# Two small attentions with scores two tiles ahead, and an fp4 layer with shared copies and another order

## The chip, the cores and the metric

One Trainium2 chip, of which the kernel uses one core. A core has TensorE (PE in the rows, its weight loads PEld), VectorE (DVE), ScalarE (ACT), GpSimd (POOL) and SyncE (SP), which issues most DMAs. The metric is device time in microseconds (us) of one execution; lower is better.

## The reference

A perceiver block in fp32 over 8 x 64 = 512 latent tokens of width 512: six residual layers, one after the other.

```python
x = x + local_attention(layernorm(x), ctx_1024)   # 16 heads of 32, rope, keys q-64..q: the first 64 of the context
x = x + self_attention(layernorm(x))              # 16 heads of 64, 64 keys in each batch
x = x + fp4_ffn(layernorm(x))                     # below
x = x + cross_attention(layernorm(x), ctx_1024)   # 1601 keys, relative positions
x = x + time_mix(x) + channel_mix(x)
x = x + small_mlp(x)
```

The first three are what matters here. Both attentions are `softmax(q k^T) v` for each batch and head and then an output product. The fp4 layer rounds blocks of 16 values to a grid of eight magnitudes, weights and activations alike:

```python
scale = max(abs(block)) / 6;  q = grid_nearest(block / scale) * sign * scale
h = silu(fp4(x) @ fp4(w_gate).T) * (fp4(x) @ fp4(w_up).T)      # 512 -> 1408
y = fp4(h) @ fp4(w_down).T                                     # 1408 -> 512
```

## The kernel before, in words

The 512 tokens are four tiles of 128 (`NT` = 4; a tile is two batches of 64). Each layer is a block: every engine gets its own instruction list, written out by hand in the order in which it is to run, and semaphores join the lists. Between two blocks all engines wait for each other. An engine runs its list strictly in order, so a wait holds up all that stands behind it.

`local_projections` (1st block) makes keys, values and queries of attention 0. At its end TensorE turns the roped queries (L213) into PSUM banks 4 to 7, one bank for each tile, and ScalarE copies them into the block-diagonal tensor `BQ` in 32 copies, eight for each tile (L231).

`small_attention` runs twice: attention 0 ("a0", masked, heads of 32) and attention 1 ("a1", heads of 64), in between `self_projections`. For each tile t:

- TensorE `scores(t)`: 16 products (L304; each fp32 product is two records in the trace) into banks 0 and 1. They hold one tile, so scores(t) waits until VectorE has read scores(t-1).
- VectorE `soften(t)`: the mask (L366, attention 0 only), the maximum (L369) and the subtraction (L370).
- ScalarE `exponentials(t)` (L409).
- VectorE `weigh(t)`: sum (L376), reciprocal, product (L380).
- TensorE `values(t)`: eight transposes (L314) into banks 2 and 3; ScalarE copies them to `pT` (L418).
- TensorE `context(t)` (L325), copied by ScalarE to `oT` (L421); TensorE `project(t)`, the output product (L128).
- VectorE `residual(t)`: adds to X (L355) and takes the moments for the next norm.

VectorE's list is weigh(t), soften(t+1), in attention 1 some rounding of the `w_up` weights ("other"), residual(t-1), then the same for t+1. ScalarE's is exponentials(t+1), the `pT` copy of t, the `oT` copy of t.

`fp4_layer` first turns both weight matrices: 22 groups of four transposes by TensorE (L939), in turn into banks 0 and 1, each copied out by ScalarE (L917), and only then free for the group after next. VectorE rounds the first tiles of the activations meanwhile (`whole`). Then comes the list `ORDER`: "turn" a rounded chunk (TensorE, copied by ScalarE in the same place of its list), "gu" one of 12 pairs of gate and up products (ScalarE then does silu, L930, VectorE the product, L892), "size" a step of the rounding on ScalarE (L694, between VectorE's `divide` and `complete`), "down" one of four output products. Chunks are X0 to X0+3 (activations), D0 to D0+3 (`w_down`) and H0 to H0+3 (h).

Of the kernel before, what the change touches and what calls it, by code (L numbers as in the profile page):

```python
# [14 lines left out]
P = 128  # L15
B, SQ, D = 8, 64, 512
SK = 1601
TOK = B * SQ
NT = TOK // P
# [117 lines left out]
    return last  # L137


def local_projections(nc, sem, s):  # L140


    with ExitStack() as ctx:
# [15 lines left out]
        def rotate(eng, ch, y, out, tmp, t):  # L159
# [7 lines left out]
            ch.link(eng.tensor_tensor(tv[:, :, 1, :], yv[:, :, 0, :], over(rope[:, 2, :], 1, NH), ALU.mult))  # L167
            return eng.tensor_tensor(out[:, t, :], out[:, t, :], tmp[:, :], ALU.add)

        block = ctx.enter_context(nc.Block())  # L170

        @block.sync
# [43 lines left out]
        @block.scalar  # L216
        def _(act):
            for t in range(NT):
                nm.scalar(act, t, bank(t), s.XT)
            for t in range(NT):  # L220
                act.wait_ge(kt_ps, t + 1)
                nc.scalar.copy(s.KT[:, 0:KC, t * P:(t + 1) * P],
                               bank(t).rearrange("p (g n) -> p g n", g=KC)).then_inc(kq_in, 1)
            act.wait_ge(bq_zero, 1)
            for t in range(NT):
                act.wait_ge(qt_ps, t + 1)
                for h in range(4):

                    rows = slice(32 * h, 32 * h + 32)
                    for b in range(2):  # L230
                        nc.scalar.copy(s.BQ[rows, h // 2:HP:2, 2 * t + b, (h % 2) * SQ:(h % 2 + 1) * SQ],  # L231
                                       bank(4 + t)[rows, :].rearrange("p (g b q) -> p g b q", g=KC, b=2)[:, :, b, :]).then_inc(kq_in, 1)

        @block.gpsimd
        def _(pool):
# [11 lines left out]
        @block.vector  # L247
        def _(dve):
            ch = Chain(dve, dv)
            dve.wait_ge(l_x, 16)  # L250
            nm.vector(dve, ch, s.X, s.XN)
            dve.wait_ge(l_kb, 16)
            for t in range(NT):
                dve.wait_ge(kv_ps, t + 1)
                nc.vector.tensor_tensor(yk[:, t, :], bank(t), s.bias["kb"][:], ALU.add).then_inc(kv_out, 1)
            dve.wait_ge(l_const, 16 * 7)
            for t in range(NT):
                dve.wait_ge(kv_ps, NT + t + 1)
                nc.vector.tensor_tensor(s.V[:, t, 0:D], bank(4 + t), s.bias["vb"][:], ALU.add).then_inc(kv_out, 1)
            for t in range(NT):  # L260
                dve.wait_ge(q_ps, t + 1)
                nc.vector.tensor_tensor(yq[:, t, :], bank(4 + t), s.bias["qb"][:], ALU.add).then_inc(q_out, 1)
                dve.wait_ge(q_out, t + 1)
                rotate(nc.vector, ch, yq, rq, tq, t).then_inc(q_roped, 1)
                dve.wait_ge(q_roped, t + 1)


def small_attention(nc, sem, s, name, dh, scale, mask, w_out, out_bias, prefetch, at, nm, pt_at=None, beside=None):

    with ExitStack() as ctx:
# [24 lines left out]
        @block.tensor  # L297
        def _(pe):
            def scores(t):
                if t >= 1:  # L300
                    pe.wait_ge(s_free if mask else shifted, t)
                for b in range(2):
                    for hp in range(HP):
                        last = nc.tensor.matmul(bank(b)[:, hp * SQ:(hp + 1) * SQ], s.BQ[:, hp, 2 * t + b, :],  # L304
                                                s.KT[:, hp // pairs_in_group, (2 * t + b) * SQ:(2 * t + b + 1) * SQ],
                                                start=True, stop=True)
                last.then_inc(s_ps, 1)

            def values(t):
                pe.wait_ge(p_ready, t + 1)  # L310
                if t >= 1:
                    pe.wait_ge(pt_out, t)
                for hp in range(HP):
                    last = nc.tensor.transpose(bank(2 + hp // 4)[:, hp % 4 * P:(hp % 4 + 1) * P],  # L314
                                               pr[:, t % 2, hp, :, :].rearrange("p b k -> p (b k)"), s.ident[:])
                last.then_inc(pt_ps, 1)

            def context(t):
                pe.wait_ge(pt_out, t + 1)
                if t >= 1:  # L320
                    pe.wait_ge(o_out, t)
                for b in range(2):
                    for h in range(NH):
                        g, r = h // per, h % per * dh
                        last = nc.tensor.matmul(bank(4 + b)[r:r + dh, g * SQ:(g + 1) * SQ],  # L325
                                                s.V[b * SQ:(b + 1) * SQ, t, h * dh:(h + 1) * dh],
                                                pT[b * SQ:(b + 1) * SQ, t % 2, h // 2, h % 2 * SQ:(h % 2 + 1) * SQ],
                                                start=True, stop=True)
                last.then_inc(o_ps, 1)

            def project(t):
                pe.wait_ge(o_out, t + 1)
                if t >= 2:
                    pe.wait_ge(x_done, t - 1)
                linear_to_tokens(nc, bank(6 + t % 2), oT, t, s.w[w_out], 0, D, groups).then_inc(y_ps, 1)

            pe.wait_ge(s.loaded[w_out], 16)
            scores(0)
            for t in range(NT):
                if t + 1 < NT:  # L340
                    scores(t + 1)
                if t >= 1:
                    project(t - 1)
                values(t)
                context(t)
            project(NT - 1)

        @block.vector
# [57 lines left out]
        def _(act):  # L406
            def exponentials(t):
                act.wait_ge(shifted, t + 1)
                nc.scalar.activation(sc[:, t % 2], sc[:, t % 2], ACT.Exp, scale=scale).then_inc(exped, 1)  # L409

            exponentials(0)
            for t in range(NT):
                if t + 1 < NT:
# [376 lines left out]
def fp4_layer(nc, sem, s, nm, after):  # L790
# [16 lines left out]
    wgT = raw.tensor("wgT", [P, KC, INNER])  # L807
    hT = raw.tensor("hT", [P, IC, TOK])
    fp4 = Fp4(nc, sem, raw, "fp4", INNER, 3)
    load_wd, dv, turned, turned_out = sem("load_wd"), sem("b5_dve_step"), sem("b5_turned"), sem("b5_turned_out")  # L810
    g_ps, u_ps, silu_done, h_done, y_ps, x_done = (sem("b5_" + n) for n in ("g_ps", "u_ps", "silu", "h_done", "y_ps", "x_done"))
    bank = s.bank
    HS = 3
# [21 lines left out]
    for name, j, _ in chunks:  # L835
        if name == "x":
            groups.append(([s.XN[:, j, c * P:(c + 1) * P] for c in range(KC)], s.XT[:, :, j * P:(j + 1) * P]))
        else:
# [5 lines left out]

    ORDER = [("turn", X0), ("gu", 0), ("gu", 1), ("turn", X0 + 1), ("gu", 2), ("size", D0), ("turn", X0 + 2), ("gu", 3), ("size", D0 + 1),
             ("gu", 4), ("turn", X0 + 3), ("gu", 5), ("size", D0 + 2), ("turn", D0), ("gu", 6), ("size", D0 + 3), ("gu", 7),
             ("turn", D0 + 1), ("gu", 8), ("size", H0), ("turn", D0 + 2), ("gu", 9), ("turn", D0 + 3), ("gu", 10), ("size", H0 + 1),
             ("turn", H0), ("gu", 11), ("turn", H0 + 1), ("size", H0 + 2), ("down", 0), ("turn", H0 + 2), ("size", H0 + 3), ("down", 1),
             ("turn", H0 + 3), ("down", 2), ("down", 3)]

    with nc.Block() as block:
        @block.sync
        def _(sp):
            sp.dma_start(wd[:], s.dram["wd"]).then_inc(load_wd, 16)
            sp.wait_ge(turned_out, ends[H0 - 1])
            sp.dma_start(s.wq[:], s.dram["w3q"]).then_inc(s.l_wq, 16)
            sp.dma_start(s.raw_wv[:], s.dram["w3v"]).then_inc(s.l_wkv, 16)
            sp.dma_start(s.raw_wk[:], s.dram["w3k"]).then_inc(s.l_wkv, 16)
# [7 lines left out]
        def _(dve):  # L866
# [31 lines left out]
                dve.wait_ge(x_done, t + 1)  # L898
                after.moments(ch, t, s.X)

            whole(X0), whole(X0 + 1), whole(X0 + 2), product(0), whole(X0 + 3), product(1), divide(D0), product(2), divide(D0 + 1)
            complete(D0), product(3), divide(D0 + 2), product(4), complete(D0 + 1), product(5), divide(D0 + 3), product(6)
            complete(D0 + 2), product(7), complete(D0 + 3), divide(H0), product(8), complete(H0), product(9), divide(H0 + 1), product(10)
            complete(H0 + 1), product(11), divide(H0 + 2), complete(H0 + 2), divide(H0 + 3), residual(0), complete(H0 + 3), residual(1)
            for t in range(2, NT):
                after.apply(dve, t - 2, s.X, s.XN)
                residual(t)
# [4 lines left out]
        def _(act):  # L912
# [3 lines left out]
                    act.wait_ge(turned, k + 1)  # L916
                    nc.scalar.copy(to, bank(k % 2)[:, 0:to.shape[1] * P].rearrange("p (c n) -> p c n", n=P)).then_inc(turned_out, 1)  # L917

            empty(range(WEIGHTS))
            for kind, k in ORDER:  # L920
                if kind == "turn":
                    empty(of_chunk(k))
# [8 lines left out]

        @block.tensor
        def _(pe):
            def turn(ks):
                for k in ks:
                    if k >= 2:
                        pe.wait_ge(turned_out, k - 1)
                    for c, src in enumerate(groups[k][0]):
                        last = nc.tensor.transpose(bank(k % 2)[:, c * P:(c + 1) * P], src, s.ident[:])  # L939
                    last.then_inc(turned, 1)  # L940
# [2 lines left out]
            for kind, k in ORDER:  # L943
# [2 lines left out]
                    turn(of_chunk(k))  # L946
                elif kind == "gu":
                    t, a, b = piece(k)
                    pe.wait_ge(turned_out, ends[X0 + t])
                    if k >= 2:  # L950
                        pe.wait_ge(silu_done, k - 1)
                        pe.wait_ge(h_done, k - 1)
                    linear_to_tokens(nc, bank(2 + k % 2), s.XT, t, wgT, a, b).then_inc(g_ps, 1)
                    linear_to_tokens(nc, bank(4 + k % 2), s.XT, t, wuT, a, b).then_inc(u_ps, 1)
                elif kind == "down":
                    pe.wait_ge(turned_out, ends[H0 + k])
                    if k >= 2:
                        pe.wait_ge(x_done, k - 1)
                    linear_to_tokens(nc, bank(6 + k % 2), hT, k, wdT, 0, D, IC).then_inc(y_ps, 1)
# [1165 lines left out]
def perceiver_kernel(nc, dram, out):  # L2125
    s = Shared()
    s.dram, s.out = dram, out
    with ExitStack() as kept:
# [33 lines left out]
        norm = lambda name: Norm(nc, sem, s, name)  # L2162
        n1, n2, n3, n4, n5, n6, n7 = (norm(f"n{k}") for k in range(1, 8))
        with nc.cleanup_on_exit():
            local_projections(nc, step, s)
            small_attention(nc, step, s, "a0_", 32, 32 ** -0.5, True, "w0o", "ob", [(n, s.w[n][:], dram[n]) for n in ("w1k", "w1q", "w1v")],
                            s.tail, n1)
            self_projections(nc, step, s, n1)
            rounding = WeightRounding(nc, step, early, s)
            small_attention(nc, step, s, "a1_", 64, 64 ** -0.5, False, "w1o", "bo",  # L2170
# [82 lines left out]
```

## Time and profile before

| | us |
|---|---|
| median of 3 runs | 1541.66 (1541.19 to 1542.73) |
| the profiled execution, its own time | 1541.65 |
| its span in the trace | 1539.5 |
| TensorE busy | 1428.5 (93%) |
| VectorE busy | 709.0 (46%) |
| ScalarE busy | 507.1 (33%) |
| GpSimd busy | 365.1 (24%) |

Stamps in us from the start of the span: projections to 66, attention 0 to 132, the next projections to 207, attention 1 to 291, the fp4 layer to 448; the rest, from cross attention on, isn't touched. The granted TensorE clock ("PEclk") is a share of 2.4 GHz: 1.00 is 2.4 GHz and 0.50 is 1.2 GHz. A row of the timeline has the start, the busy time, the engine, the line, output<-input, the shapes, the count, and in brackets how long the engine had been idle and what ended that.

### The profile page before, as it was taken

The numbers are of one execution on the slowest core, as the hardware profiler recorded it, in microseconds if no ns is written. First come the engines' busy times: TensorE is split into PE (matmuls) and PEld (weight loads), VectorE is DVE, ScalarE is ACT, GpSimd is POOL, SyncE is SP. The second block draws the span as 40 slices with busy tenths as digits, with TensorE's granted clock in tenths as the row PEclk, the third lists the DMA queues.
The fourth block names the chain that finished last, engine by engine and source line by source line (L and its number), as shares of the span: only waits on it lengthen the run. The fifth ranks groups of instructions, "written<-read, shape, count | busy, mean of one in ns | idle before, by whom it ended". The sixth has DMA issues, their size and how long they took to land. (4 is left out here: it accounts for less than half of the span.)

```text
span 1539.5 us, 26558 instructions
## 1 busy us (share of the span) xinstructions
PE 1428.5 (93%) x11152; PEld 1051.7 (68%) x11152; DVE 709.0 (46%) x1309; ACT 507.1 (33%) x835; POOL 365.1 (24%) x228
## 2 busy tenths in 40 slices
PE   7787989798989899999999999999999998997995
PEld 3565876444446688888888887888888875434773
DVE  2366868977735332223322323233223333675832
ACT  0324412322212143253333432524324344523702
POOL 6102010000021332222312231313132211315911
PEclk9778978999999999999999999999999999899997
DMA  5211210100214211121111110111112016003000
GB/s 201 102 63 76 90 42 1 76 1 0 82 62 134 66 56 55 33 62 33 51 37 57 39 55 27 62 33 56 55 34 62 23 46 243 15 0 130 0 1 27
DMA packets 49572, 88.01 MB, mean 57 GB/s; under 512 B 28584, under 2 KB 41136, under 8 KB 46128
## 3 DMA queue, kind: packets, MB, share of 16 engines
q1 hardware_dynamic: 49456, 86.32, 16.1%
q8 instruction: 90, 1.47, 0.4%
q14 instruction: 26, 0.21, 0.0%
HBM read 76.61 MB, written 9.70 MB: 56 GB/s over the span
## 5 line engine op out<-in xcount | busy, mean ns | idle before, releaser
L1257 POOL TENSOR_TENSOR ctx_hi<-ctx_raw,one 128x1536 fp32r<-128x1536 f32 (+1 forms) x32 | 91.5, 2858 | 566.0 <-DMA ctx_raw<-in_ctx 379.8
L1455 ACT COPY ET<-PS 128x512 f32<-128x512 f32 (+1 forms) x224 | 129.6, 585 | 277.0 <-PE PS L1359 201.8
L1558 DVE TENSOR_SCALAR_CACHE_REDUCE E<-PS 128x384 f32<-128x384 f32 (+1 forms) x256 | 131.8, 572 | 180.5 <-PE PS L1336 179.9
L1527 DVE TENSOR_TENSOR V<-PS,vbias 128x512 f32<-128x512 f32 (+1 forms) x104 | 71.8, 691 | 193.0 <-PE PS L1303 192.8
L1303 PE MATMUL PS<-ctx_raw_r,wk_hi 128*128 128x384 f32 (+1 forms) x512 | 128.1, 355 | 0.0
L1303 PE MATMUL PS<-wv_lo,ctx_hi 128*128 128x512 f32 (+1 forms) x416 | 127.6, 406 | 0.0
L1462 ACT ACTIVATE E<-E,peak 128x1601 f32<-128x1601 f32 x64 | 103.5, 1623 | 66.9 <-DVE peak L1563 66.9
L1359 PE MATMUL PS<-ident,E 128*128 128x128 f32 (+1 forms) x832 | 123.1, 273 | 0.4 <-issue 0.4
L1303 PE MATMUL PS<-ctx_hi,wk_hi 128*128 128x384 f32 (+1 forms) x512 | 120.6, 357 | 1.5 <-POOL ctx_raw_r L1260 1.5
L1303 PE MATMUL PS<-wv_hi,ctx_hi 128*128 128x512 f32 (+1 forms) x416 | 120.4, 411 | 0.8 <-POOL ctx_raw_r L1260 0.8
L1260 POOL TENSOR_TENSOR ctx_raw_r<-ctx_raw,ctx_hi 128x1536 fp32r<-128x1536 f32 (+1 forms) x32 | 116.9, 3654 | 2.5
L1359 PEld LDWEIGHTS PS<-ident,E 128*128 128x128 f32 (+1 forms) x832 | 101.7, 140 | 18.1 <-issue 1.1
L1303 PE MATMUL PS<-ctx_hi,wk_lo 128*128 128x384 f32 (+1 forms) x512 | 113.8, 344 | 0.0
L1303 PE MATMUL PS<-wv_hi,ctx_raw_r 128*128 128x512 f32 (+1 forms) x416 | 113.6, 395 | 0.0
L1437 ACT ACTIVATE K<-PS,kbias 128x384 f32<-128x384 f32 x96 | 55.9, 582 | 154.6 <-PE PS L1303 154.6
L110 POOL TENSOR_SCALAR rstd<-mean_var 128x1 f32<-128x1 f32 x32 | 10.4, 324 | 404.2 <-DVE mean_var L92 404.2
L1303 PEld LDWEIGHTS PS<-ctx_raw_r,wk_hi 128*128 128x128 f32 x512 | 90.0, 189 | 13.8 <-issue 11.6
L1303 PEld LDWEIGHTS PS<-wv_hi,ctx_hi 128*128 128x128 f32 (+1 forms) x416 | 71.4, 184 | 34.6 <-issue 19.1
L1303 PEld LDWEIGHTS PS<-ctx_hi,wk_hi 128*128 128x128 f32 x512 | 88.1, 189 | 10.2 <-issue 5.3
L1303 PEld LDWEIGHTS PS<-ctx_hi,wk_lo 128*128 128x128 f32 x512 | 92.7, 188 | 2.0
L1303 PEld LDWEIGHTS PS<-wv_hi,ctx_raw_r 128*128 128x128 f32 (+1 forms) x416 | 76.4, 184 | 20.0
L1303 PEld LDWEIGHTS PS<-wv_lo,ctx_hi 128*128 128x128 f32 (+1 forms) x416 | 72.3, 184 | 22.6 <-issue 6.7
(296 smaller groups left out, 2201.3 us busy)
## 6 DMA issues: line engine op xcount, KB each, us to landing
ctx_raw<-in_ctx SPq DMA_DIRECT2D x24, 768.0 KB, 4.3
ctx_raw<-in_ctx_first SPq DMA_DIRECT2D x8, 900.0 KB, 4.5
rel_scr<-rel_out SPq DMA_DIRECT2D x8, 640.0 KB, 3.7
fwk<-in_fwk SPq DMA_DIRECT2D x1, 4096.0 KB, 12.2
fwv<-in_fwv SPq DMA_DIRECT2D x1, 4096.0 KB, 13.9
corr<-rel_scr SPq DMA_DIRECT2D x64, 48.0 KB
p_scr<-E SPq DMA_DIRECT2D x16, 192.0 KB, 2.3
near<-p_scr SPq DMA_DIRECT2D x64, 48.0 KB
```

The lines of the kernel that those rows point to most:

```text
L110: nc.gpsimd.tensor_scalar(self.rstd[:, t:t + 1], self.mv[:, t, 1:2], EPS, None, ALU.add).then_inc(self.rstd_ready, 1)
L1257: nc.gpsimd.tensor_tensor(ctx_hi[r][:, :, 0:n], ctx_raw[r][:, :, 0:n], one[:].unsqueeze(1).broadcast_to([P, KC, n]), ALU.mult).then_inc(S[ ...
L1260: nc.gpsimd.tensor_tensor(ctx_lo[r][:, :, 0:n], ctx_raw[r][:, :, 0:n], ctx_hi[r][:, :, 0:n].bitcast(F32), ALU.subtract).then_inc(S["split_ ...
L1303: last = nc.tensor.matmul(*products[k], start=(k == 0), stop=(k == 2 * half - 1))
L1359: last = nc.tensor.transpose(dst[0:n, r * P:(r + 1) * P], src(4 * o + r), s.ident[:])
L1437: nc.scalar.activation(K[c][:, j, 0:n], bank(4 + NUMBER[unit] % 2)[:, 0:n], ACT.Identity, bias=kbias[:, j:j + 1]).then_inc(S["k_out_act"], 1)
L1455: nc.scalar.copy(ET[0:n, j % ET_RING, :], src[0:n, :]).then_inc(S["et_out"], 1)
L1462: nc.scalar.activation(E[:, p, :], E[:, p, :], ACT.Exp, scale=scale, bias=peak[:, p:p + 1], accum_out=total[:, p:p + 1]).then_inc(S["exped ...
L1527: v.tensor_tensor(V[0:rows, at % V_RING, :], bank(4 + NUMBER[unit] % 2)[0:rows, :], vbias[0:rows, :], ALU.add).then_inc(S["v_out"], 1)
L1558: v.tensor_scalar(E[:, p, k0:k0 + n], bank(r)[:, 0:n], 1.0, None, ALU.mult, ALU.max, accum_out=tops[:, p, c:c + 1]).then_inc(S["s_out"], 1)
```

## The change

1. **Attention 0 begun with one tile's queries.** Only the eight `BQ` copies of tile 0 stay in the first block. The 24 others stand at the head of ScalarE's list in attention 0, ahead of exponentials(0); scores(t) waits for the copies of its tile.
2. **Scores two tiles ahead, in both small attentions.** TensorE's list is written in another order. VectorE's and ScalarE's lists stay (but for the copies above).
3. **fp4 layer, shared copies.** Of the 22 weight groups, the odd ones from 7 to 21 (eight) are copied out by VectorE, in its list between whole(X0) and whole(X0+1).
4. **fp4 layer, changed order.** Some "size" steps stand elsewhere among the "turn" steps on ScalarE, and VectorE's divide and complete of the h chunks come earlier than some products.

```diff
@@ local_projections, scalar
-            for t in range(NT):
-                act.wait_ge(qt_ps, t + 1)
-                for h in range(4):
...
+            queries.scalar(act, 0)
@@ small_attention, tensor
             def scores(t):
+                if queries:
+                    queries.tensor(pe, t)
...
-            scores(0)
-            for t in range(NT):
-                if t + 1 < NT:
-                    scores(t + 1)
+            scores(0), scores(1)
+            for t in range(NT):
+                values(t)
+                if t + 2 < NT:
+                    scores(t + 2)
+                context(t)
                 if t >= 1:
                     project(t - 1)
-                values(t)
-                context(t)
             project(NT - 1)
@@ small_attention, scalar
+            if queries:
+                for t in range(1, NT):
+                    queries.scalar(act, t)
             exponentials(0)
@@ fp4_layer
-             ("turn", D0 + 1), ("gu", 8), ("size", H0), ("turn", D0 + 2), ("gu", 9), ("turn", D0 + 3), ("gu", 10), ("size", H0 + 1),
-             ("turn", H0), ("gu", 11), ("turn", H0 + 1), ("size", H0 + 2), ("down", 0), ("turn", H0 + 2), ("size", H0 + 3), ("down", 1),
+             ("turn", D0 + 1), ("gu", 8), ("turn", D0 + 2), ("size", H0), ("gu", 9), ("turn", D0 + 3), ("size", H0 + 1), ("gu", 10),
+             ("turn", H0), ("gu", 11), ("size", H0 + 2), ("turn", H0 + 1), ("down", 0), ("size", H0 + 3), ("turn", H0 + 2), ("down", 1),
+    by_vector = range(7, WEIGHTS, 2)
...
-            whole(X0), whole(X0 + 1), whole(X0 + 2), product(0), whole(X0 + 3), product(1), divide(D0), product(2), divide(D0 + 1)
+            whole(X0)
+            for k in by_vector:
+                to = groups[k][1]
+                dve.wait_ge(turned, k + 1)
+                nc.vector.tensor_copy(to, bank(k % 2)[:, 0:to.shape[1] * P].rearrange("p (c n) -> p c n", n=P)).then_inc(turned_out_dve, 1)
+            whole(X0 + 1), whole(X0 + 2), product(0), whole(X0 + 3), product(1), divide(D0), product(2), divide(D0 + 1)
...
-            complete(D0 + 2), product(7), complete(D0 + 3), divide(H0), product(8), complete(H0), product(9), divide(H0 + 1), product(10)
-            complete(H0 + 1), product(11), divide(H0 + 2), complete(H0 + 2), divide(H0 + 3), residual(0), complete(H0 + 3), residual(1)
+            complete(D0 + 2), product(7), complete(D0 + 3), divide(H0), product(8), complete(H0), divide(H0 + 1), product(9), complete(H0 + 1)
+            divide(H0 + 2), product(10), complete(H0 + 2), product(11), divide(H0 + 3), residual(0), complete(H0 + 3), residual(1)
```

TensorE's list in attention 0 before, from its first scores on (`KT,BQ` are scores, `ident,XT` values, `a_pT,V` context, `w0o,a_oT` the output product; x16 is one tile's scores):

```order
L304 MATMUL PS<-KT,BQ 128x64 x32
L314 MATMUL PS<-ident,XT 128x128 x8
L325 MATMUL PS<-a_pT,V 32x64 x32
L304 MATMUL PS<-KT,BQ 128x64 x16
L128 MATMUL PS<-w0o,a_oT 128x512 x4
L314 MATMUL PS<-ident,XT 128x128 x8
L325 MATMUL PS<-a_pT,V 32x64 x32
```

The same place of the changed kernel:

```order
L322 MATMUL PS<-KT,BQ 128x64 x32
L332 MATMUL PS<-ident,XT 128x128 x8
L322 MATMUL PS<-KT,BQ 128x64 x16
L343 MATMUL PS<-a_pT,V 32x64 x32
L332 MATMUL PS<-ident,XT 128x128 x8
L322 MATMUL PS<-KT,BQ 128x64 x16
L343 MATMUL PS<-a_pT,V 32x64 x32
L128 MATMUL PS<-w0o,a_oT 128x512 x4
L332 MATMUL PS<-ident,XT 128x128 x8
```

scores(2) has moved ahead of context(0), and project(0) from ahead of values(1) to behind context(1). Attention 1 reads the same with `w1o`.

ScalarE's list in the fp4 layer before, from silu of pair 8 on (`fp_grid` is a size step, `wdT` and `hT` are copies of turned chunks):

```order
L930 ACTIVATE silu_gate_2148<-PS 128x384
L694 ACTIVATE fp_grid_2141<-fp_q_2138 128x1408
L917 COPY wdT<-PS 128x4x128 x2
L917 COPY wdT<-PS 128x3x128
L930 ACTIVATE silu_gate_2146<-PS 128x512
```

The same place of the changed kernel:

```order
L961 ACTIVATE silu_gate_2152<-PS 128x384
L948 COPY wdT<-PS 128x4x128 x2
L948 COPY wdT<-PS 128x3x128
L715 ACTIVATE fp_grid_2145<-fp_q_2142 128x1408
L961 ACTIVATE silu_gate_2150<-PS 128x512
```

The copies of chunk D0+2 now stand ahead of the size step of H0, which waits for VectorE's divide(H0).

## Rows read from the trace of the kernel before

**Rows 1.** Lines of VectorE, 66 to 132 us; behind the bars: busy and mean, idle before
```profile
L366 DVE TENSOR_TENSOR XN<-PS,mask 128x1024 f32<-128x1024 f32 x4 | 4.9, 1225 | 27.9 <-PE PS L304 27.9
```

**Rows 2.** Windows: span, busy of PE, PEld, DVE, ACT, POOL, PEclk, DMA share, GB/s
```profile
66.00:81.00 15.00, 13.40 (x62) 13.24 (x62) 6.36 (x6) 1.06 (x1) 4.93 (x4) 0.50 0.93 374
227.00:237.00 10.00, 10.00 (x97) 9.88 (x97) 4.75 (x7) 2.38 (x3) 0.00 (x0) 0.50 0.00 0
```

**Rows 3.** Lines of TensorE, 66 to 101.9 us
```profile
L128 PE MATMUL PS<-w0o,a_oT 128*128 128x512 f32 x8 | 5.9, 903 | 0.0
...
L325 PE MATMUL PS<-a_pT,V 64*32 64x64 f32 x64 | 1.5, 311 | 4.2 <-ACT a_pT L418 4.2
```

**Rows 4.** Timeline of attention 0 and the copies ahead of it
```profile
55.53 10.45 ACT L231 COPY BQ<-PS 32x256 f32<-32x256 f32 x32
...
66.28 7.06 PE L304 MATMUL PS<-KT,BQ 128*128 128x64 f32 x32 [9.51 <-PEq L143]
...
96.78 1.23 DVE L366 TENSOR_TENSOR XN<-PS,mask 128x1024 f32<-128x1024 f32 x1 [7.36 <-PE PS L304]
...
100.55 1.06 ACT L409 ACTIVATE XN<-XN 128x1024 f32<-128x1024 f32 x1 [10.65 <-DVE XN L370]
...
102.03 0.69 DVE L355 TENSOR_TENSOR X<-PS,X 128x512 f32<-128x512 f32 x1 [1.51 <-PE PS L128]
...
112.37 0.69 DVE L355 TENSOR_TENSOR X<-PS,X 128x512 f32<-128x512 f32 x1
...
115.42 1.23 DVE L380 TENSOR_TENSOR XT<-XN,a_sm 128x1024 f32<-128x1024 f32 x1
...
119.97 0.69 DVE L355 TENSOR_TENSOR X<-PS,X 128x512 f32<-128x512 f32 x1 [3.33 <-PE PS L128]
...
129.01 0.69 DVE L355 TENSOR_TENSOR X<-PS,X 128x512 f32<-128x512 f32 x1 [5.50 <-PE PS L128]
```

**Rows 5.** Timeline of attention 1
```profile
226.86 3.32 PE L325 MATMUL PS<-a_pT,V 64*64 64x64 f32 x64 [3.00 <-ACT a_pT L418]
...
236.99 8.81 PE L128 MATMUL PS<-w1o,a_oT 128*128 128x512 f32 x16
...
249.42 0.69 DVE L355 TENSOR_TENSOR X<-PS,X 128x512 f32<-128x512 f32 x1
...
253.24 7.08 PE L128 MATMUL PS<-w1o,a_oT 128*128 128x512 f32 x16
...
265.32 10.02 PE L128 MATMUL PS<-w1o,a_oT 128*128 128x512 f32 x16 [1.11 <-ACT a_oT L421]
265.74 0.69 DVE L355 TENSOR_TENSOR X<-PS,X 128x512 f32<-128x512 f32 x1
...
279.65 0.69 DVE L355 TENSOR_TENSOR X<-PS,X 128x512 f32<-128x512 f32 x1
```

**Rows 6.** Timeline of the fp4 layer, the weight groups
```profile
297.04 1.17 PE L939 MATMUL PS<-ident,wg 128*128 128x128 f32 x8 [0.16 <-ACT wgT L917]
...
297.73 1.10 ACT L917 COPY wgT<-PS 128x512 f32<-128x512 f32 x2 [0.23 <-PE PS L939]
```

**Rows 7.** Timeline of the fp4 layer, from size(H0) on
```profile
373.95 1.38 ACT L694 ACTIVATE fp_grid<-fp_q 128x1408 f32<-128x1408 f32 x1 [5.32 <-DVE fp_q L681]
...
375.86 0.90 PE L939 MATMUL PS<-ident,wd 128*128 128x128 f32 x3 [4.30 <-ACT wdT L917]
376.55 5.51 PE L128 MATMUL PS<-wgT,XT 128*128 128x512 f32 x8
...
401.43 1.61 DVE L677 TENSOR_REDUCE fp_scale<-h 128x88 f32<-128x1408 f32 x1
...
402.34 9.61 PE L128 MATMUL PS<-wdT,hT 128*128 128x512 f32 x22
...
405.95 1.38 ACT L694 ACTIVATE fp_grid<-fp_q 128x1408 f32<-128x1408 f32 x1 [2.93 <-DVE fp_q L681]
...
412.36 1.09 PE L939 MATMUL PS<-ident,h 128*128 128x128 f32 x8 [0.41 <-DVE h L703]
```

More of the change, by code:

```diff
@@ L137, in linear_to_features, with __init__, scalar, tensor @@
     return last
+class Queries:
+    def __init__(self, nc, s, turned, ready):
+        self.nc, self.s, self.turned, self.ready = nc, s, turned, ready
+    def scalar(self, act, t):
+        act.wait_ge(self.turned, t + 1)
+        for h in range(4):
+            rows = slice(32 * h, 32 * h + 32)
+            for b in range(2):
+                self.nc.scalar.copy(self.s.BQ[rows, h // 2:HP:2, 2 * t + b, (h % 2) * SQ:(h % 2 + 1) * SQ],
+                                    self.s.bank(4 + t)[rows, :].rearrange("p (g b q) -> p g b q", g=KC, b=2)[:, :, b, :]).then_inc(self.ready, 1)
+    def tensor(self, pe, t):
+        pe.wait_ge(self.ready, 8 * (t + 1))
 def local_projections(nc, sem, s):
@@ L168, in rotate @@
             return eng.tensor_tensor(out[:, t, :], out[:, t, :], tmp[:, :], ALU.add)
+        queries = Queries(nc, s, qt_ps, sem("bq0_in"))
         block = ctx.enter_context(nc.Block())
@@ L224, in _ @@
             act.wait_ge(bq_zero, 1)
-            for t in range(NT):
-                act.wait_ge(qt_ps, t + 1)
-                for h in range(4):
[L229 to L232, printed above, removed]
+            queries.scalar(act, 0)
         @block.gpsimd
@@ L265, in _, with small_attention @@
                 dve.wait_ge(q_roped, t + 1)
-def small_attention(nc, sem, s, name, dh, scale, mask, w_out, out_bias, prefetch, at, nm, pt_at=None, beside=None):
+    return queries
+def small_attention(nc, sem, s, name, dh, scale, mask, w_out, out_bias, prefetch, at, nm, pt_at=None, beside=None, queries=None):
     with ExitStack() as ctx:
@@ L809, in fp4_layer @@
     fp4 = Fp4(nc, sem, raw, "fp4", INNER, 3)
-    load_wd, dv, turned, turned_out = sem("load_wd"), sem("b5_dve_step"), sem("b5_turned"), sem("b5_turned_out")
+    load_wd, dv, turned = sem("load_wd"), sem("b5_dve_step"), sem("b5_turned")
+    turned_out, turned_out_dve = sem("b5_turned_out"), sem("b5_turned_out_dve")
     g_ps, u_ps, silu_done, h_done, y_ps, x_done = (sem("b5_" + n) for n in ("g_ps", "u_ps", "silu", "h_done", "y_ps", "x_done"))
@@ L846, in fp4_layer @@
              ("gu", 4), ("turn", X0 + 3), ("gu", 5), ("size", D0 + 2), ("turn", D0), ("gu", 6), ("size", D0 + 3), ("gu", 7),
-             ("turn", D0 + 1), ("gu", 8), ("size", H0), ("turn", D0 + 2), ("gu", 9), ("turn", D0 + 3), ("gu", 10), ("size", H0 + 1),
-             ("turn", H0), ("gu", 11), ("turn", H0 + 1), ("size", H0 + 2), ("down", 0), ("turn", H0 + 2), ("size", H0 + 3), ("down", 1),
+             ("turn", D0 + 1), ("gu", 8), ("turn", D0 + 2), ("size", H0), ("gu", 9), ("turn", D0 + 3), ("size", H0 + 1), ("gu", 10),
+             ("turn", H0), ("gu", 11), ("size", H0 + 2), ("turn", H0 + 1), ("down", 0), ("size", H0 + 3), ("turn", H0 + 2), ("down", 1),
              ("turn", H0 + 3), ("down", 2), ("down", 3)]
+    by_vector = range(7, WEIGHTS, 2)
+    copied_by_scalar = lambda end: sum(k not in by_vector for k in range(end))
+    copied_by_vector = lambda end: sum(k in by_vector for k in range(end))
     with nc.Block() as block:
@@ L854, in _ @@
             sp.dma_start(wd[:], s.dram["wd"]).then_inc(load_wd, 16)
-            sp.wait_ge(turned_out, ends[H0 - 1])
+            sp.wait_ge(turned_out, copied_by_scalar(ends[H0 - 1]))
             sp.dma_start(s.wq[:], s.dram["w3q"]).then_inc(s.l_wq, 16)
@@ L917, in empty @@
                     nc.scalar.copy(to, bank(k % 2)[:, 0:to.shape[1] * P].rearrange("p (c n) -> p c n", n=P)).then_inc(turned_out, 1)
-            empty(range(WEIGHTS))
+            empty(k for k in range(WEIGHTS) if k not in by_vector)
             for kind, k in ORDER:
@@ L933, in _, with wait_copied @@
         def _(pe):
+            def wait_copied(pe, k):
+                if k in by_vector:
+                    pe.wait_ge(turned_out_dve, copied_by_vector(k + 1))
+                else:
+                    pe.wait_ge(turned_out, copied_by_scalar(k + 1))
             def turn(ks):
@@ L936, in turn @@
                     if k >= 2:
-                        pe.wait_ge(turned_out, k - 1)
+                        wait_copied(pe, k - 2)
                     for c, src in enumerate(groups[k][0]):
@@ L948, in _ @@
                     t, a, b = piece(k)
-                    pe.wait_ge(turned_out, ends[X0 + t])
+                    pe.wait_ge(turned_out, copied_by_scalar(ends[X0 + t]))
+                    pe.wait_ge(turned_out_dve, len(by_vector))
                     if k >= 2:
@@ L955, in _ @@
                 elif kind == "down":
-                    pe.wait_ge(turned_out, ends[H0 + k])
+                    pe.wait_ge(turned_out, copied_by_scalar(ends[H0 + k]))
                     if k >= 2:
@@ L2164, in perceiver_kernel @@
         with nc.cleanup_on_exit():
-            local_projections(nc, step, s)
+            queries = local_projections(nc, step, s)
             small_attention(nc, step, s, "a0_", 32, 32 ** -0.5, True, "w0o", "ob", [(n, s.w[n][:], dram[n]) for n in ("w1k", "w1q", "w1v")],
-                            s.tail, n1)
+                            s.tail, n1, queries=queries)
             self_projections(nc, step, s, n1)
```

## The prediction

> **What bounds the kernel now.** I read the page for the engines' shares, then windows of the granted clock over both attentions, then the timeline engine by engine from 53 to 450 us. TensorE is busy 93% of the span, but not in the stages that the change touches. In attention 0 VectorE waits 27.9 us for scores alone [rows 1]: it is a chain across three engines that sets the time there. The change goes at those waits. But each tile's scores(t+1) and project(t-1) run today while VectorE and ScalarE soften, and that cover is what the new order gives away.
>
> The second thing to see is the clock. During the first two scores of attention 0, and during scores and context of attention 1, TensorE is busy nearly all the time and still granted 0.50 (1.2 GHz) [rows 2]: scores alone do not raise it. It rises in a project: project(0) of attention 1 takes 8.81 us for 16 records, the same work 7.08 later, and project(2), which begins cold after short idle spells, 10.02 [rows 5]. In attention 0 a project (eight records) takes 5.9 cold [rows 3] and half of 7.08, about 3.6, warm.
>
> **The sum, part by part.** "x0" is the start of residual(0), and so on: the points where VectorE's list waits for a project, before and after. VectorE's list isn't touched, so a later x is a later everything.
>
> *Attention 0, up to x0.* The first block ends with 32 `BQ` copies of 0.33 us, 10.45 together, and scores begin at 66.28 [rows 4]. Eight remain, 2.6 us: scores(0) begins at about 58.4, 7.8 earlier. The other 24 run on ScalarE till 66.3; the first exponential can't come sooner than scores(0) (6.2 to 7.06) and soften (3.77, from 96.78 to 100.55 [rows 4]), 68.4, so the moved copies are hidden, and tile 1's are there at 61. Without that cover they would cost up to 7.8. From 58.4 TensorE's list is the chain: scores(0) 6.2 (the idle spell is now short, so it may start warm), mask 1.3, scores(1) to (3) 7.06 each, context(0) and (1) 1.5 each, values(0) and (1) about 2 each (eight transposes take 1.17 warm [rows 6], twice that less the wait in it), project(0) 5.9: 41.6, less some 1.0 for the overlap of one group with the next. x0 is at 99 against 102.03 [rows 4]: **-3**.
>
> *x0 to x1.* Before, 10.34 us [rows 4]. New: residual and weigh 4.28 (112.37 to 116.65), soften 3.77, exponential 1.06, the `pT` copy 1.0, context(2) 1.0 to 1.5, project(1) 3.6 to 5.9 [rows 3, 4], hand-offs 0.2: one after the other, for project(t-1) now stands behind context(t), context(t) needs the `pT` copy, and that stands on ScalarE behind exponentials(t+1). 14.9 to 17.7, that is +4.6 to +7.4.
>
> *x1 to x2.* Before 7.60. New: 4.28, values 1.1 to 2, copy 1.0, context 1.0 to 1.5, project 3.6 to 5.9, 0.2: 11.2 to 14.9, +3.6 to +7.3. *x2 to x3*: before 9.04, because project(3) waited for values, copy and context of tile 3; now project(3) follows project(2) at once, 3.6 to 5.9: -5.4 to -3.1. Behind x3 nothing changes. Attention 0 in all: from -0.2 to +8.6, middle about +4. I take **+3**: the first scores may keep the warm clock for a while.
>
> *Attention 1.* Up to scores(1) nothing changes. Soften(1) ends at about 224.7 (226.86 less the exponential and the copy [rows 5]). From there, cold: scores(2) 7.06, context(0) 3.32, values(1) 2, scores(3) 7.06, context(1) 3.32, project(0) 8.81, less 0.7 of overlap: x0 at 255.6 instead of 249.42 [rows 5], +6.2; +4.4 if the project took 7.08, +7.4 if 10.02. That soften(2) comes some 5 us sooner buys nothing, since weigh(2) stands behind residual(0). *x0 to x1*: 16.32 before. New: 4.28, soften 2.5 (no mask), 1.06, 1.0, context 1.9 to 3.3, project 7.08 to 10.02, 0.2: 18.1 to 22.4, +1.8 to +6.1. VectorE's rounding (16.32 less 4.28 and 2.5, so 9.5) lies beside that wait and is shorter than it. *x1 to x2*: 13.91 before; new 4.28, values 1.1 to 2, 1.0, context 1.9 to 3.3, project 7.08 to 10.02, 0.2: 15.6 to 20.8, +1.7 to +6.9. Behind x2 VectorE is the bound before and after. In all +7.9 to +20.4; I take **+14**, near the middle, because TensorE idles for residual and weigh and again for exponential and copy in each tile, and project(2), which came cold after such spells, is the 10.02 row. The Trainium skill (TensorE: Matmul & The Clock Gate, HAM oscillation) says that idle gaps between bursts send TensorE back to half rate, and the next burst then starts cold; its rule speaks against this order. The trace agrees with 10.02 against 7.08, and without the rule the term would be the warm end, +7.9.
>
> *fp4 layer, shared copies.* A pair of groups comes every 1.33 us (297.04 and the 1.17 and 0.16 behind it [rows 6]). ScalarE is not the bound: it is busy 1.10 and waits 0.23 for TensorE. The loop is one bank's: four transposes 0.6, hand-over 0.1, copy 0.55, hand-over 0.05 to 0.1. With VectorE on the odd bank the loop keeps its length, and a VectorE operation of the width takes 0.69 [rows 4], so from group 7 on 7.5 pairs at 1.33 to 1.45: 0 to +0.9, I take **+0.4**. VectorE's whole(X0+1) and (X0+2) come some 5 us later than before; the first is wanted only after two pairs of products (14 us), and the delay of product(0) runs out within eight products.
>
> *fp4 layer, order.* Before, ScalarE sits in size(H0) until VectorE's divide(H0) ends at 373.95; the `wdT` copies stand behind it, and TensorE waits 4.30 and then runs cold, 5.51 for what takes 3.6 (half of 7.08) [rows 5, 7]. Now the copies go first: -4.3 and -1.9, and 0.3 on the transposes: -6.5. What is late next is VectorE's chain. divide takes 4.52 (401.43 to 405.95), complete 4.9 (407.4 to 412.3) [rows 7]. From 375.4: complete(H0) to 380.3, divide(H1) 384.8, size 386.2, complete(H1) 391.1, divide(H2) 395.6, size(H2) 397.0. ScalarE's copies of turn(H1) now stand behind that size, so down(0) begins at about 398.1 instead of 402.34. complete(H2) ends at 401.9, divide(H3) with a product at 407.0, size(H3) at 408.4, and turn(H2)'s copies behind it let down(1) go at 409.8, against 412.36 + 1.7 before. The rest is TensorE alone. So -4.2; with another cold start in the wait at 396, down to -2.5; at best -4.8. I take **-4.2**.
>
> Sum: -3 and +6 in attention 0 (+3), +14, +0.4, -4.2: **+13**. The profiled execution took 1541.65 us (span 1539.5), within 0.01 of the median, so 1555.
>
> **Rivals.**
> - *The clock stays up and two-ahead pays* (slower becomes faster). If TensorE keeps 2.4 GHz through attention 0, scores are 3.6 to 3.8 and x0 is at about 88.5 on VectorE's chain (58.4, three softens and two weighs with their exponentials, then context and project), -13.5; with the warm ends +4.6, +3.6, -5.4 that is -10.7. Attention 1 in the same state gains about 7 up to x0 and loses 3.5: -3.5. With the fp4 layer -3.8: -18, 1523.5. For it: TensorE's idle spell before scores(0) shrinks from 9.51 us to under 2. Against: 0.50 in both rows of scores [rows 2], and spells of idleness that get longer. It decides when scores(0) and scores(1) of attention 0 are both granted 1.00. 8 in 100.
> - *All warm ends, without that*: -0.2, +7.9, -4.2: +3.5, and with a start half warm about 0. 8 in 100 for within 0.2%, 3 more for faster.
> - *Cold ends throughout*: +8.6, +20.4, -2.5: +26, 1568. 9 in 100.
> - *Sharing doubles the copying*: if a pair then came at TensorE's own pace (two groups of 0.43, half the gapless part of 1.17), 7.5 pairs save 0.45 each, -3.4, so 1551. The wait of ScalarE for TensorE in [rows 6] is against it. 5 in 100. The Trainium skill (TensorEngine Tiling (Array Packing), PSUM Bottleneck) advises to use both ScalarE and VectorE to empty PSUM; here it would be right only if copying were the bound.
>
> **The numbers.** Forecast with its own range 1546 to 1563: 67 in 100. Cases below zero change: 11, within 0.2% (3.1 us, about what a measurement of this kernel can tell): 8, slower: 81. The range for 8 in 10 reaches down to 1543 and up to 1564.
>
> **What would show it.** Right: scores(0) at 58 to 59 us; VectorE idle before residual(0) and (1) in both attentions, for 5 to 15 us each, ended by L128; nearly none left before soften; clock 0.50 at the start of most projects; the 4.30 wait gone and down(0) some 4 us nearer to the layer's start; the pair of weight groups still 1.3 to 1.45. Wrong: projects of attention 1 at 7.1 us each; or x0 of attention 0 more than 5 us earlier.

## The result, and the profile after

The changed kernel takes 1553.55 us (median of 6 runs, 1544.04 to 1556.71) against 1541.8 (6 runs, 1541.19 to 1542.73): a ratio of 1.0062, interval 1.0043 to 1.008. It is slower, by 12 us between the medians and by 9.6 (6.6 to 12.3) by the ratio, against the 13 forecast. Its runs differ by 12.7 us, where those of the kernel before differ by 1.5 here and by 5.8 in a larger set (17 runs, beside e1). They line up with the granted clock of the whole run:

```
us        1544.04  1548.28  1553.37  1553.74  1554.65  1556.71
clock      0.957    0.955    0.950    0.950    0.951    0.947
```

The profiled execution is the fastest of them, so its trace shows the mildest case. A second set of runs of the same kernel (e10 below) was profiled in one of 1559.47 us at 0.945. No execution near the median has a trace. The table puts both beside the kernel before; a stage is the stretch from TensorE's first operation in a block to its first in the next.

| us | before | changed, 1544.04 | changed again, 1559.47 |
|---|---|---|---|
| up to scores(0) of attention 0 | 66.3 | 59.9 | 59.0 |
| attention 0 | 66.2 | 69.4 | 78.4 |
| projections of attention 1 | 75.0 | 75.8 | 76.0 |
| attention 1 | 84.7 | 93.1 | 99.8 |
| fp4 layer | 155.8 | 152.1 | 151.3 |

Lines of VectorE in attention 0 and then in attention 1 of the changed kernel (behind the second bar: idle before, and what ended it):

```profile
L384 DVE TENSOR_TENSOR XN<-PS,mask 128x1024 f32<-128x1024 f32 x4 | 4.9, 1222 | 8.6 <-PE PS L322 8.6
L373 DVE TENSOR_TENSOR X<-PS,X 128x512 f32<-128x512 f32 x4 | 2.8, 690 | 25.2 <-PE PS L128 25.2
...
L387 DVE TENSOR_REDUCE a_mx<-PS 128x16 f32<-128x1024 f32 x4 | 4.9, 1223 | 6.8 <-PE PS L322 6.8
L373 DVE TENSOR_TENSOR X<-PS,X 128x512 f32<-128x512 f32 x4 | 2.8, 689 | 15.8 <-PE PS L128 15.8
```

The waits for scores that the change went for did fall, from 27.9 [rows 1] to 8.6 (half of the fall is the earlier start: the wait ahead of the first mask went from 17.32 to 7.79). But residual, which waited 1.5, 0, 3.3 and 5.5 us for its project before [rows 4], now waits 25.2 in attention 0, and 15.8 in attention 1, where it had not waited at all. The timeline of attention 0 shows how (ScalarE, TensorE and VectorE mixed):

```profile
56.78 2.60 ACT L153 COPY BQ<-PS 32x256 f32<-32x256 f32 x8
...
59.66 7.84 ACT L153 COPY BQ<-PS 32x256 f32<-32x256 f32 x24 [0.28 <-PEq L164]
...
59.86 5.20 PE L322 MATMUL PS<-KT,BQ 128*128 128x64 f32 x32 [1.84 <-PEq L164]
...
68.87 1.06 ACT L427 ACTIVATE XN<-XN 128x1024 f32<-128x1024 f32 x1 [1.38 <-DVE XN L388]
...
75.03 3.97 PE L322 MATMUL PS<-KT,BQ 128*128 128x64 f32 x32
...
91.62 0.69 DVE L373 TENSOR_TENSOR X<-PS,X 128x512 f32<-128x512 f32 x1 [6.77 <-PE PS L128]
...
95.96 1.93 PE L332 MATMUL PS<-ident,XT 128*128 128x128 f32 x8 [4.45 <-DVE XT L398]
...
101.59 1.54 PE L343 MATMUL PS<-a_pT,V 64*32 64x64 f32 x64 [3.71 <-ACT a_pT L439]
...
108.46 0.69 DVE L373 TENSOR_TENSOR X<-PS,X 128x512 f32<-128x512 f32 x1 [8.90 <-PE PS L128]
```

The copies are hidden: the 24 end at 67.5, the first exponential waits for VectorE until 68.87. Between 91.62 and 108.46 the two engines take turns: TensorE idles 4.45 us for residual and weigh, 3.71 for exponential and copy, its context runs cold and its project (5.28 us) begins cold, and VectorE idles 8.90 for the project. Here scores(2) was granted the full clock early (3.97 us), and scores(3) and project(0) had it too (3.76 and 3.70), so x0 fell at 91.6. In the 1559.47 us execution the same scores, begun at nearly the same stamp, ran cold, scores(3) as well (6.93), and x0 fell at 99.4, where the prediction had put it:

```profile
74.94 6.97 PE L322 MATMUL PS<-KT,BQ 128*128 128x64 f32 x32
...
99.36 0.69 DVE L373 TENSOR_TENSOR X<-PS,X 128x512 f32<-128x512 f32 x1 [13.18 <-PE PS L128]
...
116.60 0.69 DVE L373 TENSOR_TENSOR X<-PS,X 128x512 f32<-128x512 f32 x1 [9.30 <-PE PS L128]
...
130.45 0.69 DVE L373 TENSOR_TENSOR X<-PS,X 128x512 f32<-128x512 f32 x1 [9.56 <-PE PS L128]
...
133.90 0.69 DVE L373 TENSOR_TENSOR X<-PS,X 128x512 f32<-128x512 f32 x1
```

The fp4 layer of the changed kernel (1544.04), the answers to [rows 6] and [rows 7]:

```profile
307.93 0.69 DVE L931 COPY wuT<-PS 128x512 f32<-128x512 f32 x1 [0.75 <-PE PS L976]
...
309.37 0.69 DVE L931 COPY wuT<-PS 128x512 f32<-128x512 f32 x1 [0.75 <-PE PS L976]
...
404.55 0.55 PE L976 MATMUL PS<-ident,h 128*128 128x128 f32 x3 [2.01 <-ACT hT L948]
```

Pairs of weight groups come every 1.44 us instead of 1.33. The wait ahead of pair 9 and its cold 5.51 us are gone (3.60), and the new wait of 2.01 for ScalarE ahead of down(0) is the one foreseen.

### The profile page after: what moved, and what is told of

Its sections match the earlier page's. It is cut to its first block and busy times, and to the rows that moved or that the text cites. A ratio compares the mean times of both kernels' runs of the same rounds, so it can differ in the third digit from the quotient of the medians.

```text
span 1541.7 us, 26574 instructions
## 1 busy us (share of the span) xinstructions
PE 1427.9 (93%) x11152; PEld 1051.5 (68%) x11152; DVE 713.8 (46%) x1317; ACT 502.2 (33%) x827; POOL 365.1 (24%) x228
## 3 DMA queue, kind: packets, MB, share of 16 engines
q1 hardware_dynamic: 49456, 86.32, 16.2%
## 5 line engine op out<-in xcount | busy, mean ns | idle before, releaser
L110 POOL TENSOR_SCALAR rstd<-mean_var 128x1 f32<-128x1 f32 x32 | 10.4, 325 | 413.0 <-DVE mean_var L92 413.0
L1341 PEld LDWEIGHTS PS<-ctx_raw_r,wk_hi 128*128 128x128 f32 x512 | 90.0, 189 | 13.8 <-issue 11.6
L1341 PEld LDWEIGHTS PS<-wv_hi,ctx_hi 128*128 128x128 f32 (+1 forms) x416 | 71.4, 184 | 34.6 <-issue 20.8
## 6 DMA issues: line engine op xcount, KB each, us to landing
fwk<-in_fwk SPq DMA_DIRECT2D x1, 4096.0 KB, 12.3
```

Source lines behind the costliest of these rows:

```text
L110: nc.gpsimd.tensor_scalar(self.rstd[:, t:t + 1], self.mv[:, t, 1:2], EPS, None, ALU.add).then_inc(self.rstd_ready, 1)
L1341: last = nc.tensor.matmul(*products[k], start=(k == 0), stop=(k == 2 * half - 1))
```

## The experiments

Each was timed in five rounds with the kernel before on the same chip; the ratio is to that, with its interval. e1 to e4 shared one chip, e5 to e8 a second, e9 to e11 a third; across these groups the ratios are compared, not the times.

**e1_old_order.** TensorE's list of both attentions put back.

```diff
-            scores(0), scores(1)
...
+            scores(0)
             for t in range(NT):
+                if t + 1 < NT:
+                    scores(t + 1)
+                if t >= 1:
+                    project(t - 1)
                 values(t)
-                if t + 2 < NT:
-                    scores(t + 2)
                 context(t)
-                if t >= 1:
-                    project(t - 1)
```

> The changed kernel with TensorE's old order in both small attentions (scores one tile ahead, project(t-1) ahead of values(t)); queries, shared copies and fp4 order stay changed. Theory (the loss is project(t-1) behind context(t)): the loss is gone and the gains of the other parts stand bare, -7.8 for the earlier start, -4 for the fp4 order, up to +1 for the shared copies: 1530 us, 1526 to 1535. Rival 1 (the 24 moved copies hold up the first exponential): 1538 to 1545. Rival 2 (the fp4 parts lose): above 1536 with the fp4 layer longer than before.

Measured 1531.25 us, 0.9932 (0.9915 to 0.9948). The other three parts gain 10.6 us against the kernel before; TensorE's list turns that into a loss. Both rivals fall: the time is under their ranges, and the fp4 layer in its trace is 151.4 us long against 155.8.

**e2_ahead_only.** The same edit of the list, alone, on the kernel before.

> The kernel before with only TensorE's list of the small attentions changed (two ahead, project behind context). Theory: all of the loss and none of the gains: +10 in attention 0, +14 in attention 1, so 1566 us, 1555 to 1573, with a wide spread from run to run because the cold stretches fall differently. Rival (two-ahead by itself is neutral or pays, the loss is in the other parts): 1542 or less.

Measured 1564.62 us, 1.015 (1.0132 to 1.0168): a loss of 22.8 us, near the 24 that the theory puts on it. With e4, e5 and e6 below (-3.2, 0 and -7.6 by their ratios) the four parts add up to +12, what the medians give for the whole change. The foreseen spread wasn't there (1563.57 to 1565.76 in four runs).

**e3_project_first.** The changed kernel with one call moved.

```diff
             for t in range(NT):
+                if t >= 1:
+                    project(t - 1)
                 values(t)
                 if t + 2 < NT:
                     scores(t + 2)
                 context(t)
-                if t >= 1:
-                    project(t - 1)
```

> The changed kernel with one call moved: project(t-1) stands at the head of the tile's work, then values(t), scores(t+2), context(t). Scores stay two ahead. Theory: the cover is back and VectorE no longer waits for scores nor projects: attention 0 about 19 us shorter than before the change (8 of it the start), attention 1 about 2 shorter, fp4 3.5: 1517 us, 1511 to 1525. Rival (scores(t+2) ahead of context(t) is what costs): 1550 or more, as the changed kernel. Second rival (only the cold clock costs, whatever the order): above 1535.

Measured 1517.09 us, 0.9853 (0.983 to 0.9876). Residual in attention 0 of this kernel:

```profile
84.80 0.69 DVE L373 TENSOR_TENSOR X<-PS,X 128x512 f32<-128x512 f32 x1
...
94.49 0.69 DVE L373 TENSOR_TENSOR X<-PS,X 128x512 f32<-128x512 f32 x1 [1.56 <-PE PS L128]
...
101.83 0.69 DVE L373 TENSOR_TENSOR X<-PS,X 128x512 f32<-128x512 f32 x1 [3.06 <-PE PS L128]
```

The waits are back at the size of before, and x0 to x1 is 9.7 us instead of 16.8. Two tiles ahead is worth having as soon as project keeps its cover: 14 us better than e1 by the medians, 12 by the ratios. One of its five runs took 1525.91 us; it has no trace.

**e4_fp4_order_only.** Part 4 alone on the kernel before (the last two hunks of the diff).

> The kernel before with only the new ORDER and VectorE's new order of the h chunks in the fp4 layer. Theory: the 4.30 us wait ahead of pair 9 and its cold start are gone, down(0) some 4 us sooner: 1537.6 us, 1537 to 1540. Rival (VectorE's chain takes it all back): 1541 to 1543.

Measured 1539.36 us over 12 runs, 0.9979 (0.9968 to 0.9991): by the ratio a gain of 3.2 us (1.4 to 4.9), under the 4.2 but with it inside the interval. Its trace has pair 9 without the wait. The fp4 layer in it lasts 152.4 us (294.05 to 446.41) against 155.8. Some 1.7 us are lost again in the way that the prediction allowed for: behind the new wait of 2.01 us down(0) begins cold and takes 11.26 us, where it takes 9.61 before and in both traces of the changed kernel.

**e5_share_only.** Part 3 alone.

> The kernel before with only the shared copies of the weight groups. Theory (one bank's loop of transposes and copy sets the pace, not ScalarE): pairs come every 1.33 to 1.45 us as before, the layer is 0 to 1 us longer: 1542.3 us, 1541 to 1544. Rival (copying was the bound): pairs every 0.9 us, 1538.5.

Measured 1541.72 us, 1.000 (0.999 to 1.001). Nothing gained and nothing lost that can be told in the total. Its trace has pairs every 1.44 us and not every 0.9, so the rival falls, and the stretch from the first weight group to the end of the last takes 16.2 us instead of 15.6: +0.6 against the +0.4 forecast, too small for the total to show.

**e6_queries_only.** Part 1 alone.

> The kernel before with only attention 0 begun with one tile's queries. Theory: scores(0) 7.8 us sooner and the 24 copies hidden behind scores(0) and soften(0): 1534 us, 1530 to 1537. Rival (the copies delay the first exponential): 1538 or more.

Measured 1534.79 us, 0.9951 (0.9936 to 0.9967): 6.8 us by the medians, 7.6 (5.1 to 9.9) by the ratio. In its trace scores(0) stands at 59.40, 6.9 us earlier.

**e7_best.** e3 with the copies of the weight groups back on ScalarE (`by_vector = range(0)`).

> Queries begun early, scores two ahead with project(t-1) at the head of the tile, the new fp4 order, and all weight groups copied by ScalarE as before the change. Theory: as the same kernel with shared copies (1517.09) or up to 1 us faster: 1516.5 us, 1512 to 1521.

Measured 1520.46 us, 0.9857 (0.9839 to 0.9875). As e3 within the intervals; the shared copies make no difference here either that can be told. Its profiled execution (1521.82) had scores(2) of attention 0 cold (6.97 us, x0 at 89.54), that of e3 mostly warm (4.25, x0 at 84.80): the clock again, and not the copies. Both beat both kernels.

**e8_project_mid.** project(t-1) between scores(t+2) and context(t).

> The changed kernel with project(t-1) between scores(t+2) and context(t): still behind scores(t+2) and values(t), but no longer behind the pT copy that waits for exponentials(t+1). Theory: project(t-1) runs while VectorE softens, so most of the cover is back, but less than at the head, where it also stands ahead of scores(t+2): 1532 us, 1525 to 1540. Rival (any place behind values(t) loses it all): 1550 or more.

Measured 1532.92 us, 0.9945 (0.993 to 0.996). In front of context(t) the project no longer waits for the exponentials of the next tile, and 18 us come back by the ratios (22 against the second set of the changed kernel); at the head of the tile it is worth 14 more.

**e11_one_ahead_late.** Scores one tile ahead as before, project(t-1) behind context(t) as in the change.

```diff
-            scores(0), scores(1)
+            scores(0)
             for t in range(NT):
+                if t + 1 < NT:
+                    scores(t + 1)
                 values(t)
-                if t + 2 < NT:
-                    scores(t + 2)
                 context(t)
```

> The changed kernel with scores only one tile ahead as before the change, but project(t-1) left behind context(t). Theory (project's place is the loss, two-ahead alone costs nothing): the loss stays in full, 1558 us, 1550 to 1564, against 1531.25 with project(t-1) ahead of values(t). Rival (scores(t+2) ahead of context(t) is part of the loss): 1540 or less.

Measured 1559.2 us, 1.0112 (1.0098 to 1.0125), 28 us behind e1 (by the ratios as well), from which only project's place differs. The changed kernel took 1557.6 on the same chip (e10), so with project late the two-ahead scores cost nothing. With e3 this settles it: with scores one ahead or two, the place of project is the whole loss.

**e9_keep_warm.** Four extra products behind project(0) and project(1) of each attention, into a bank that the next project overwrites; nobody reads them.

```diff
+            def keep_warm(t):
+                if t >= 2:
+                    pe.wait_ge(x_done, t - 1)
+                linear_to_tokens(nc, bank(6 + t % 2), oT, t - 1, s.w[w_out], 0, D, 4)
...
                 if t >= 1:
                     project(t - 1)
+                if 1 <= t < NT - 1:
+                    keep_warm(t)
```

> The changed kernel, and behind project(0) and project(1) of each small attention four products more of the same size, whose result nobody reads, into the bank that is next to be overwritten. They lie where TensorE idles 4.45 us for residual and weigh, and take 3.6 us warm. Theory (the serial order costs most, the cold clock some of it): contexts and projects are more often warm, some 7 us off, 1547 us, 1541 to 1551. Rival 1 (cold clock is nearly all of the loss): 1535 or less. Rival 2 (the clock is no part of it): 1552 to 1558.

Measured 1552.38 us, 1.006 (1.0047 to 1.0074), 5.2 below the changed kernel's 1557.6 on the same chip (next). That misses the forecast: 1552.38 lies above its range and inside that of rival 2 (the clock is no part of it), so the total can't decide between them; the trace can. Context(2), residual(1), context(3) and residual(2) in attention 0:

```profile
101.38 1.54 PE L343 MATMUL PS<-a_pT,V 64*32 64x64 f32 x64 [4.54 <-ACT a_pT L446]
...
108.62 0.69 DVE L380 TENSOR_TENSOR X<-PS,X 128x512 f32<-128x512 f32 x1 [9.28 <-PE PS L128]
...
115.15 0.99 PE L343 MATMUL PS<-a_pT,V 64*32 64x64 f32 x64 [1.10 <-ACT a_pT L446]
...
119.88 0.69 DVE L380 TENSOR_TENSOR X<-PS,X 128x512 f32<-128x512 f32 x1 [6.98 <-PE PS L128]
```

x1 to x2 is 11.26 us here and 15.65 in attention 1 (269.32 to 284.97), the warm ends of the prediction (11.2 and 15.6) to a tenth, where the changed kernel had 13.8 and 19.9. x0 to x1 stayed long in both (17.2 and 21.0). The rows show why: the extra products fill the gap ahead of values (4.45 us, now 1.02), and behind x0 a second gap remains, for exponential and copy, 4.54 us and 3.29 in attention 1, and context then runs cold (1.54 and 3.32). Behind x1 that second gap is 1.10, and context runs warm (0.99 and 1.91). The two warm stretches also show the serial order without the cold clock: before the change x1 to x2 took 7.60 and 13.91 us, so +3.7 and +1.7 are the order and +2.6 and +4.2 the clock. The intervals of the two ratios (this and the next) overlap, so the 5 us in the total are likely, not certain.

**e10_after_again.** The changed kernel once more.

> The changed kernel once more, for the spread of its runs beside the others on the same chip: median 1553, between 1544 and 1558. If its fastest and slowest runs differ by the clock alone, the time falls as the granted clock of the whole run rises.

Measured 1557.6 us over 6 runs (1548.29 to 1560.0), 1.0088 (1.0065 to 1.011). Clock and time go together again: 1548.29 at 0.954, 1551.42 at 0.953, 1556.34 at 0.948, 1558.86 to 1560.0 at 0.945 and 0.946. The median lies inside the expected 1544 to 1558, near its top; three of the six runs are above 1558.

## Why the prediction held

*Bound and mechanism.* Right in the order of the work. The chain across three engines was lengthened where the prediction said, by project(t-1) behind context(t) behind the `pT` copy behind exponentials(t+1); e11 and e3 isolate it from both sides.

*The terms*, against the two profiled executions of the changed kernel:

| term | forecast | 1544.04 | 1559.47 |
|---|---|---|---|
| attention 0 with its start | +3 | -3.3 | +4.9 |
| projections of attention 1 | 0 | +0.8 | +1.1 |
| attention 1 | +14 | +8.4 | +15.1 |
| fp4 layer | -3.8 | -3.7 | -4.5 |

The terms of the two executions add up to +2.2 and +16.6 us (the whole times say +2.4 and +17.8); the forecast of 13 and the median of 12 lie in between. The execution of 1559.47 us is near the forecast by its terms, and by its steps too: scores(0) at 59.0 (58.4), x0 at 99.4 (99), x0 to x1 17.2 (14.9 to 17.7), x1 to x2 13.9 (11.2 to 14.9); in attention 1 x0 to x1 20.9 (18.1 to 22.4) and x1 to x2, 280.87 to 300.75, 19.9 (15.6 to 20.8). Its +15.1 in attention 1 is made up otherwise than the +14: x0 was only 4.7 us later instead of 6.2 (scores(0) took 3.76 us against 5.02 before, where the prediction said that nothing changes), and the two stretches behind it 4.5 and 6.0 more, above the middle of their ranges.

*A sign of being wrong that came.* The prediction named x0 of attention 0 more than 5 us earlier as such a sign. In the 1544.04 us execution it was 10.4 us earlier (91.62 against 102.03), and attention 0 with its start gained 3.3 us instead of losing 3. That was one of six runs by its time, and the only one of them with a trace. So that the median came within 1.3 us of the forecast is in part luck: it depends on how many executions took which course.

*A small miss.* x2 to x3 in attention 0 took 3.5 us in both executions (rows 130.45 and 133.90 above), just under the 3.6 to 5.9 of the prediction. project(3) ran warm right behind project(2), and no wait stands ahead of residual(3): between the two residuals VectorE was busy, but for 0.46 us, with the moments and the norm of three tiles, which the prediction left out.

*The clock.* The prediction took near the middle between warm and cold because of the spells of idleness, 4.45 and 3.71 us, and they were there. Its evidence was thinner than it says: the cold project(2) of 10.02 us in the kernel before came behind spells of 1.10 and 1.11 us, not of 4. Its reading that scores alone do not raise the clock and a project does is not general: in the 1544.04 us execution the granted clock rose from 0.50 to 1.00 in the middle of scores(2) of attention 0 (at 75 to 76 us) and of scores(3) of attention 1 (at 232 to 233), ahead of any project. The rival in which the clock stays up did not come by its own condition, since scores(0) and (1) of attention 0 ran at 0.50 for most of their time (5.20 and 7.06 us), but in part the clock did stay up: scores(2) and (3) took 3.97 and 3.76 us, and x0 was 8 us sooner than in the other execution. What decides between the two courses is open. That "1553.55" is a median over such a mixture is likely from the spread, and not shown, as only two executions have traces. Of the twelve runs of both sets eleven lie in the likeliest case's range of 1546 to 1563, and 1544.04 below it.

The Trainium skill (TensorE: Matmul & The Clock Gate, HAM oscillation) says that idle gaps send TensorE back to half rate. This trace agrees: project(0) of attention 0 ran warm (3.70 us), and behind the 4.45 us gap the transposes take 1.93 us instead of the 1.09 of the tile before; e9, which fills the 4.45 us gaps, brings to their warm length the two of four stretches that have no second long gap.

*Shared copies.* Right as a mechanism (0.75 us of VectorE's time between copies is waiting for TensorE), at the upper end in size: 1.44 us for a pair against 1.33 to 1.45. ScalarE and VectorE each wait 0.75 us of the 1.44 for TensorE, and TensorE 0.35 for VectorE, so no engine is the bound but the loop through a bank. The Trainium skill (TensorEngine Tiling (Array Packing), PSUM Bottleneck) advises to let both engines empty PSUM once a faster TensorE makes the copies the bottleneck; they weren't here, and e5's ratio is 1.000.

*fp4 order.* The mechanism was right in each step: the 4.30 us wait gone, the new one of 2.01 for ScalarE ahead of down(0). Forecast -4.2; the stage measured -3.7 and -4.5 with the shared copies, and e4 -3.2 (-4.9 to -1.4) by its ratio and -3.4 by the stage of its trace, with the cold start of down(0) for which the prediction had allowed down to -2.5.

## What to carry to other kernels

When a list is reordered to bring one operation forward, write down for each operation that moved back who waits for it, and on what it now waits itself: here a product that nobody seemed to need soon was the input of the next link. Two tiles ahead and cover for the output product don't exclude each other; the order project(t-1), values(t), scores(t+2), context(t) has both and is 1.5% faster than the kernel before. And price a chain that alternates between engines at both clocks: its idle spells can bring it to the lower one, and one program can take either course from run to run.

## What the runs showed of the hardware beyond that

- A busy TensorE isn't always a warm one. In the window below (attention 0 of the 1559.47 us execution; busy time of PE, PEld, DVE, ACT and POOL, then the granted clock) it was busy 32.62 of 33 us and was granted 0.52 in the mean, 1.2 GHz; the rise came in project(0), between 97 and 98 us. The clock can also fall in the middle of busy work: in the 1544.04 us execution TensorE was busy without a break from 60 to 65 us, in scores(0), granted 0.98 in the mean up to 62 and 0.50 from there.

```profile
66.00:99.00 33.00, 32.62 (x248) 28.63 (x248) 15.42 (x15) 6.90 (x10) 0.00 (x0) 0.52 0.29 122
```

- One program, two courses: scores(2) of attention 0 began at 75.03 in one execution and at 74.94 in another and took 3.97 and 6.97 us. e3 and e8 have the same list up to there: begun at 74.86 and 74.85, it took 4.25 and 6.97. What tips it was not tried.
- A cold start of one stretch varies without a change to its work: the weight groups of the fp4 layer began cold in six traces compared, and the clock rose about 3 us later before the change, in e1, e4 and e5 and in the 1559.47 us execution, but only 6.7 us later in that of 1544.04 (298.14 to 304.9, 32 transposes in 6.87 us). So the faster of the two traced executions of the changed kernel had the longer cold start there.
